# Finding eight top-512 thresholds in a fused attention and expert layer: scores turned so that a partition holds 256 scores of one expert

## The reference

```python
xf = z.reshape(-1, 256)                        # 4096 tokens
k = 4096 // 8                                  # 512 tokens for each of 8 experts
scores = (jnp.tanh(xf @ gate_w.T) + 1.0) * 0.5 # 4096 x 8, between 0 and 1
vals, idx = jax.lax.top_k(scores.T, k)         # for each expert its 512 highest scores
y = _layernorm(xf[flat_idx].reshape(k, n, d), ln_gamma, ln_beta)
h = gelu(einsum('knd,nfd->knf', y, fc1s) + b1s)
o = (einsum('knf,ndf->knd', h, fc2s) + b2s) * vals.T[:, :, None]
out = xf.at[flat_idx].add(o.reshape(k * n, d))
```

## Time and profile before

| | |
|---|---|
| median of 3 runs | 1595.7 us |
| profiled execution, its own time | 1597.86 us |
| span of its trace | 1596.1 us |
| PE busy | 1514.2 us (95%) |
| DVE busy | 1123.7 us (70%) |
| ACT busy | 910.7 us (57%) |
| POOL busy | 546.1 us (34%) |
| threshold rounds, first test to last | 1271.81 to 1304.93 us |
| mean granted PE clock | 0.965 |

### The profile page before, as it was taken

One profiled execution on the slowest core, in us unless ns is written; L12 is line 12 of the kernel. 1 busy time (PEld: TensorE's weight loads), 2 busy tenths in 40 slices (PEclk: granted clock), 3 DMA queues, 4 the chain that ended last, 5 costly groups with the idle time before them and its releaser, 6 DMA issues. The chain is left out here.

```text
span 1596.1 us, 26481 instructions
## 1 busy us (share of the span) xinstructions
PE 1514.2 (95%) x9025; PEld 733.7 (46%) x9025; DVE 1123.7 (70%) x3056; ACT 910.7 (57%) x1754; POOL 546.1 (34%) x1009
## 2 busy tenths in 40 slices
PE   8899999999999999999999999999999868999997
PEld 4433444444444444444444444444443424666664
DVE  6878887887787788778877877788781274554441
ACT  2167777677766777677777677777767301112111
POOL 4122333442343225233433442451121302443342
PEclk9599999999999999999999999999999877999999
DMA  6776662855376556737672855377300211343432
GB/s 136 155 135 104 127 88 77 121 105 106 104 104 136 87 101 124 123 84 109 120 122 83 115 105 105 94 102 141 42 3 3 87 38 38 101 108 100 123 90 50
DMA packets 82490, 155.46 MB, mean 97 GB/s; under 512 B 13012, under 2 KB 46420, under 8 KB 82356
## 3 DMA queue, kind: packets, MB, share of 16 engines
q1 hardware_dynamic: 76212, 145.25, 47.0%
q0 software_dynamic: 6144, 8.52, 3.1%
HBM read 96.52 MB, written 53.08 MB: 94 GB/s over the span
## 5 line engine op out<-in xcount | busy, mean ns | idle before, releaser
L829 ACT ACTIVATE probs<-bank_ps 128x512 f32<-128x512 f32 (+1 forms) x1408 | 730.1, 579 | 247.9 <-PE bank_ps L613 239.0
L920 DVE TENSOR_REDUCE chunk_max<-bank_ps 128x1 f32<-128x512 f32 x1024 | 653.5, 683 | 144.0 <-PE bank_ps L652 140.2
L652 PE MATMUL bank_ps<-k_stack,q_stack 62*128 62x512 f32 (+3 forms) x1536 | 536.3, 432 | 7.4 <-DVE chunk_max L920 4.1
L613 PE MATMUL bank_ps<-q_stack,k_stack 64*128 64x512 f32 (+3 forms) x1536 | 512.8, 423 | 25.7 <-ACT probs L829 22.1
L652 PEld LDWEIGHTS bank_ps<-k_stack,q_stack 62*128 62x128 f32 x1536 | 248.2, 191 | 372.4 <-DVE chunk_max L920 202.2
L923 DVE CUSTOM_DVE_ANT_0 masked<-bank_ps,causal 128x128 bf16<-128x128 f32 (+3 forms) x512 | 232.9, 485 | 62.4 <-PE bank_ps L652 58.8
L631 PE MATMUL out_ps<-probs,v_cross 128*32 128x512 f32 x2048 | 275.7, 610 | 0.0
L613 PEld LDWEIGHTS bank_ps<-q_stack,k_stack 64*128 64x128 f32 x1536 | 234.5, 189 | 83.2 <-ACT probs L829 76.3
L1093 POOL TENSOR_TENSOR pool_idle<-pool_idle 128x1 f32<-128x1 f32 x292 | 56.4, 193 | 582.5 <-ACT probs L829 386.1
L1406 ACT ACTIVATE h<-h_ps,b1T 128x512 f32<-128x512 f32 x64 | 44.0, 687 | 254.5 <-PE h_ps L1352 220.4
L1352 PE MATMUL h_ps<-ff_yT,w1T 128*128 128x512 f32 x256 | 122.6, 615 | 1.0 <-DVE ff_yT L1419 1.0
(11 more groups left out here) (165 smaller groups left out, 1384.0 us busy)
## 6 DMA issues: line engine op xcount, KB each, us to landing
parts_dram<-parts SPq DMA_DIRECT2D x70, 512.0 KB, 2.7
k_stack<-parts_dram SPq DMA_DIRECT2D x180, 192.0 KB, 11.6
q_stack<-parts_dram SPq DMA_DIRECT2D x180, 128.0 KB, 10.5
w1T<-in_L_ffn_fc1s SPq DMA_DIRECT2D x8, 1024.0 KB, 5.0
w2T<-in_L_ffn_fc2s SPq DMA_DIRECT2D x8, 1024.0 KB, 7.3
z_rows<-z_sb SPq DMA_DIRECT2D x8, 528.0 KB, 3.1
x_sb<-in_x SPq DMA_DIRECT2D x8, 512.0 KB, 3.8
ctxT<-in_ctx SPq DMA_DIRECT2D x8, 512.0 KB, 4.1
```

The lines of the kernel that those rows point to most:

```text
L613: mm = pe.matmul(bank_of(turn)[:, of.at:of.end], k_stack[base:base + SIDE, g, pair, of.keys:of.keys + P], q_stack[base:base + SIDE, g, pai ...
L652: return pe.matmul(bank[:, 0:n], q_stack[base:base + MAX_ROWS, g, pair, qc:qc + P], k_stack[base:base + MAX_ROWS, g, pair, k0:k0 + n], sta ...
L829: nc.scalar.activation(probs[:, buffer(u, i, p), side, columns], bank_of(("score", g, i, p, side))[:, columns], ACT.Exp, scale=SCALE)\
L920: nc.vector.tensor_reduce(dst, bank[:, 0:n], AX.X, ALU.max).then_inc(max_done, 1)
```

## The change: what it does

The scores are turned once, by two fp32 PE transposes of every second column of `s_all` and a DVE copy out of PSUM, into `by_expert`, in which a partition holds 256 scores of one expert and 16 neighbouring partitions hold one expert. A level is then one number a partition, and the three tests of a round are three DVE instructions of 256 elements, each with its level as a scalar per partition and each summing its own result into one column of `counts`. One PE product of three columns with `block_ones` (ones within blocks of 16 partitions) sums over an expert. `passed` compares with 511.5 and sums the three results (`passes`); `levels` and `bottom` follow from it. `levels_ahead`, the part of the next levels that does not need the count, is issued while PE works. At the end `bottom_wide` and a PE transpose turn the result back, and a copy picks `low`. The products of ones after the count are in 5 rounds in place of 13 (the eighth to the twelfth), and none follows the last count. The identity is no longer written again: the attention's tile is kept.

```diff
@@ attention(...), feed_forward(...): both take ident as an argument; in program():
+        ident = stack.enter_context(nc.sbuf_tensor("ident", [P, P], F32))
@@ feed_forward, shapes
-    TILE_STEP = 4
+    SHARE = P // E
+    VALUES = NTOK // SHARE
...
-        reached_ps = h_ps[:, 0, 0:TESTS * E * TILE_STEP]
+        by_expert_ps = transpose_ps[:, 0, 0:VALUES]
+        reached_ps = h_ps[:, 0, 0:TESTS]
+        low_ps = transpose_ps[:, 1, 0:P]
@@ tensor queue
+            flat_scores = s_all[:].rearrange("p e t -> p (e t)")
+            for c in range(VALUES // P):
+                mm = pe.transpose(by_expert_ps[:, c * P:(c + 1) * P], flat_scores[:, c::VALUES // P], ident[:])
+            mm.then_inc(turned, 1)
+            pe.wait_ge(consts, 1)
             pe.wait_ge(pool_set, 1)
             for r in range(ROUNDS):
                 pe.wait_ge(tested, r + 1)
-                for t in range(0, TILES, TILE_STEP):
-                    mm = pe.matmul(reached_ps, ones[:], reached[:, :, :, t:t + TILE_STEP], start=t == 0,
-                                   stop=t == TILES - TILE_STEP)
-                mm.then_inc(counted, 1)
-                multiply_ones(ONES_PER_ROUND)
+                pe.matmul(reached_ps, block_ones[:], counts[:], start=True, stop=True).then_inc(counted, 1)
+                if ROUNDS - ROUNDS_WITH_ONES <= r + 1 < ROUNDS:
+                    multiply_ones(ONES_PER_ROUND)
+            pe.wait_ge(bottom_set, ROUNDS + 1)
+            pe.transpose(low_ps, bottom_wide[:], ident[:]).then_inc(low_full, 1)
@@ vector queue (the old rounds are printed above, L1522 to L1548)
+            step = [0.5 * 0.25 ** r for r in range(ROUNDS + 1)]
+            nc.vector.memset(bottom[:], 0.0).then_inc(bottom_set, 1)
+            for n in range(TESTS):
+                nc.vector.memset(multiples[:, n:n + 1], n + 1.0)
+            for n in range(TESTS):
+                init = nc.vector.memset(levels[:, n:n + 1], (n + 1) * step[0])
+            init.then_inc(levels_set, 1)
+            dve.wait_ge(turned, 1)
+            nc.vector.tensor_copy(by_expert[:], by_expert_ps).then_inc(laid, 1)
+            dve.wait_ge(laid, 1)
             for r in range(ROUNDS):
+                dve.wait_ge(levels_set, r + 1)
+                for n in range(TESTS):
+                    test = nc.vector.tensor_scalar(reached[:, n, :], by_expert[:], levels[:, n:n + 1], None, ALU.is_ge,
+                                                   ALU.add, accum_out=counts[:, n:n + 1])
+                test.then_inc(tested, 1)
+                dve.wait_ge(bottom_set, r + 1)
+                nc.vector.scalar_tensor_tensor(out=levels_ahead[:], in0=multiples[:], scalar=step[r + 1],
+                                               in1=bottom[:].broadcast_to([P, TESTS]), op0=ALU.mult, op1=ALU.add)\
+                    .then_inc(ahead_set, 1)
                 dve.wait_ge(counted, r + 1)
+                nc.vector.tensor_scalar(passed[:], reached_ps, K - 0.5, None, ALU.is_ge, ALU.add, accum_out=passes[:])\
+                    .then_inc(passes_set, 1)
+                dve.wait_ge(passes_set, r + 1)
                 if r < ROUNDS - 1:
+                    dve.wait_ge(ahead_set, r + 1)
+                    nc.vector.scalar_tensor_tensor(out=levels[:], in0=passes[:].broadcast_to([P, TESTS]), scalar=step[r],
+                                                   in1=levels_ahead[:], op0=ALU.mult, op1=ALU.add).then_inc(levels_set, 1)
+                    nc.vector.scalar_tensor_tensor(out=bottom[:], in0=passes[:], scalar=step[r], in1=bottom[:],
+                                                   op0=ALU.mult, op1=ALU.add).then_inc(bottom_set, 1)
+                else:
+                    nc.vector.scalar_tensor_tensor(out=bottom_wide[:], in0=passes[:].broadcast_to([P, P]), scalar=step[r],
+                                                   in1=bottom[:].broadcast_to([P, P]), op0=ALU.mult, op1=ALU.add)\
+                        .then_inc(bottom_set, 1)
+            dve.wait_ge(low_full, 1)
+            nc.vector.tensor_copy(low[:], low_ps.rearrange("p (e n) -> p e n", e=E)[:, :, 0]).then_inc(low_set, 1)
+            dve.wait_ge(low_set, 1)
@@ GpSimd queue
-            nc.gpsimd.memset(ident[:], 0.0)
+            nc.gpsimd.memset(block_ones[:], 1.0)
...
             pool.wait_ge(pool_set, 1)
+            in_block = lambda sign: [[sign * SHARE, E], [0, SHARE]]
+            nc.gpsimd.affine_select(out=block_ones[:], in_=block_ones[:], compare_op=ALU.is_ge, fill=0.0, base=0,
+                                    pattern=in_block(-1), channel_multiplier=1).then_inc(block_step, 1)
+            pool.wait_ge(block_step, 1)
+            nc.gpsimd.affine_select(out=block_ones[:], in_=block_ones[:], compare_op=ALU.is_ge, fill=0.0, base=SHARE - 1,
+                                    pattern=in_block(1), channel_multiplier=-1).then_inc(consts, 1)
...
-            nc.gpsimd.affine_select(out=ident[:], in_=ident[:], compare_op=ALU.not_equal, fill=1.0, base=0,
-                                    pattern=[[-1, P]], channel_multiplier=1).then_inc(consts, 1)
@@ constants
-ONES_PER_ROUND = 4
+ONES_PER_ROUND, ROUNDS_WITH_ONES = 4, 5
```

More of the change, by code:

```diff
@@ L257, in head_place, with attention @@
     return SIDE * (h % SIDES), h // SIDES
-def attention(nc, x, ctx_in, w, z_rows, out, parts_dram, shift_dram, s_all, x1, z_sb, z_out, base_out):
+def attention(nc, x, ctx_in, w, z_rows, out, parts_dram, shift_dram, s_all, x1, z_sb, ident, z_out, base_out):
     B, T, C = x.shape
@@ L307, in attention @@
         minus_half = sb("minus_half", [P, NT])
-        ident = sb("ident", [P, P])
         causal = sb("causal", [P, T])
@@ L1202, in _, with feed_forward @@
             second_norm(B - 1)
-def feed_forward(nc, w, z_rows, out, s_all, z_out, base_out):
+def feed_forward(nc, w, z_rows, out, s_all, ident, z_out, base_out):
     E, C, F = w["fc1s"].shape
@@ L1246, in feed_forward @@
         pool_idle = sb("ff_pool_idle", [P, 17]); dve_idle = sb("ff_dve_idle", [P, 1])
-        ident = sb("ff_ident", [P, P])
+        block_ones = sb("block_ones", [P, P], BF16)
         ones = sb("ones", [P, P], BF16); upto = sb("upto", [P, P], BF16)
@@ L1250, in feed_forward @@
         token = sb("token", [P, 2, TILES], BF16)
-        low = sb("low", [P, E]); levels = sb("levels", [P, 1 + TESTS, E]); steps = sb("steps", [P, 1 + TESTS, E])
-        counts = sb("counts", [P, 1 + TESTS, E]); passed = sb("passed", [P, 1 + TESTS, E])
-        reached = sb("reached", [P, TESTS, E, TILES], BF16)
+        low = sb("low", [P, E])
+        by_expert = sb("by_expert", [P, VALUES]); reached = sb("reached", [P, TESTS, VALUES], BF16)
+        multiples = sb("multiples", [P, TESTS]); levels = sb("levels", [P, TESTS]); levels_ahead = sb("levels_ahead", [P, TESTS])
+        counts = sb("counts", [P, TESTS], BF16); passed = sb("passed", [P, TESTS]); passes = sb("passes", [P, 1])
+        bottom = sb("bottom", [P, 1]); bottom_wide = sb("bottom_wide", [P, P])
         count = sb("count", [P, E])
@@ L1275, in feed_forward @@
         above_ps = o_ps[:, 1, 0:E * TILES]
-        reached_ps = h_ps[:, 0, 0:TESTS * E * TILE_STEP]
+        by_expert_ps = transpose_ps[:, 0, 0:VALUES]
+        reached_ps = h_ps[:, 0, 0:TESTS]
+        low_ps = transpose_ps[:, 1, 0:P]
         w1_in = sem("w1_in"); w2_in = sem("w2_in"); b2_in = sem("b2_in"); small_in = sem("small_in")
-        consts = sem("ff_consts"); pool_set = sem("ff_pool_set")
-        tested = sem("tested"); counted = sem("counted"); round_step = sem("round_step")
+        consts = sem("ff_consts"); pool_set = sem("ff_pool_set"); block_step = sem("block_step")
+        turned = sem("turned"); laid = sem("laid"); low_full = sem("low_full")
+        tested = sem("tested"); counted = sem("counted"); levels_set = sem("levels_set")
+        bottom_set = sem("bottom_set"); ahead_set = sem("ahead_set"); passes_set = sem("passes_set"); low_set = sem("low_set")
         route = sem("route"); route_ps = sem("route_ps")
@@ L1519, in _ @@
             wide = lambda tile: tile[:].unsqueeze(2).broadcast_to([P, E, TILES])
[L1522 to L1528, removed]
-            for r in range(ROUNDS):
[L1530 to L1534, removed]
-                dve.wait_ge(counted, r + 1)
[L1536 to L1545, removed]
-                if r < ROUNDS - 1:
-                    nc.vector.tensor_tensor(levels[:], low[:].unsqueeze(1).broadcast_to([P, 1 + TESTS, E]), steps[:],
-                                            ALU.add).then_inc(round_step, 1)
@@ L1716, in program @@
         z_sb = stack.enter_context(nc.sbuf_tensor("z_sb", [P, T // P, C + E], F32))
+        ident = stack.enter_context(nc.sbuf_tensor("ident", [P, P], F32))
         z_out = stack.enter_context(nc.semaphore("z_out"))
         base_out = stack.enter_context(nc.semaphore("base_out"))
-        attention(nc, x, ctx_in, w, z_rows, out, parts_dram, shift_dram, s_all, x1, z_sb, z_out, base_out)
-        feed_forward(nc, w, z_rows, out, s_all, z_out, base_out)
```

(2 more changed lines are left out.)

## The result

The changed kernel takes 1587.99 us, the median of 5 runs (1583.82 to 1589.78), against 1595.7 us before (by then the median of 5 runs, and the same); the ratio is 0.9942 with a 95% interval from 0.9919 to 0.9964. Forecast was 1587.0 in a range from 1579 to 1594. Timed once more on another occasion beside 11 runs of the kernel before (median 1594.94), it took 1587.5 us, ratio 0.9949 (0.9934 to 0.9964). So the medians lie 7.4 and 7.7 us apart, on the edge of the 0.5% that one measurement can tell; the two intervals together reach from 5.7 to 12.9 us, and both exclude no change.

What follows compares the result with a forecast made beforehand. The threshold search was taken to bound the start of the feed-forward part, one for one. Start +0.64, twelve rounds -9.1, last test +0.3, tail -0.5 sum to -8.7 us: 1595.7 becomes 1587.0 us, range 1579 to 1594.

Steps and rivals of the forecast that it cites:

- The bound: Feed-forward start: ACT and POOL wait on the threshold search, whose time is added to the end one for one.
- Start: Block's start until the first test: two fp32 transposes and a PSUM copy delay it by 0.64 us.
- Three tests: DVE tests of each round: 1.28 us at one element per step, spacing 0.40 us, where one test took 0.96.
- Rival 1: Search tests take two elements per step: three take 0.89 us, -12.5 us in all, 1583.2 us; chance 0.24.
- One product and two small operations: Rest of each round behind the tests: product 0.28 us, passed 0.20, levels 0.19; bottom and levels_ahead are hidden.
- The allowance of 0.05 for one more wait: DVE's queue in each round: one additional wait, put at 0.05 us, bounds 0 and 0.1.
- Ones: PE products of ones in five rounds: cost nothing at 2.00 us a round, PE being free after about 1.85 us.
- Tail: From the end of the last test to count: 2.33 us against 2.83, that is -0.5 us.
- Sum: Whole kernel: +0.64 - 9.1 + 0.3 - 0.5 = -8.7 us, giving 1587.0 us on the median.
- Later clock effects: After the gather, transposes and first expert: PE's clock falling at another moment adds about 2.5 us on either side.
- The range: Whole kernel: 1579 us (tests at two elements, kind clock) to 1594 us (small operations not hidden, unkind clock).
- Rival 3: Search tests do not overlap and run slowly: three take 2.15 us, +2.6 us in all, 1598.3 us; chance 0.05.

Runs made afterwards that it cites:

- e2: Changed kernel with the three tests as plain comparisons without sums, counts constant: round 1.56 to 1.57 us, search 24.05 us; whole time not given.
- e4: Changed kernel with levels_ahead issued behind passed and bottom ahead of levels, so neither is covered: round 2.19 us, search 31.03 us; whole time not given.
- e7: Changed kernel with the turned scores in bf16, sums unused, counts constant: round 1.97 us; whole time not given.
- e8: Changed kernel with 44 products of ones ahead of the first transposes in place of 32, profiled: search 28.22 us; whole time not given.
- e9: Same kernel as e8 (changed kernel, 44 products of ones in place of 32), timed: 1588.26 us, ratio 0.9949 to the kernel before.
- e3: Changed kernel with a semaphore wait between the three tests of a round: round 2.22 us, search 31.93 us; whole time not given.
- e5: Changed kernel with four products of ones after each of the 13 counts: rounds 1.96 to 1.97 us, search 28.44 us; whole time not given.
- e1: Kernel before, unchanged, profiled again: search 35.00 us; whole time not given.
- e6: Kernel before without products of ones in its rounds: mean round 2.86 us, search 38.31 us; whole time not given.

## Why the prediction was right, and where it was off

*The bound.* Right: the search is added to the end one for one; POOL's and ACT's waits shrank by 9.0 us each, and no later wait swallowed it. In this pair the first expert took 0.9 us longer after (19.1 against 18.2), which is the clock effect below.

*Start.* Forecast +0.64 us. Measured first test 1.13 us into the block against 0.33: +0.80 us, and +0.61 in e2, e4, e7, e8 and e9 (0.94). The two transposes depend on the clock at that moment: one takes 0.28 to 0.36 us in e8 and 0.42 to 0.46 in the profile after. The step had one number for them, which is near that of the full clock.

*Three tests.* Forecast 1.28 us with a spacing of 0.40; measured 1.27 and 0.40. This step decided the sum, and the choice of the accumulating row over the quicker one was right. The rule of the Trainium skill (VectorE: DVE Perf Modes, "The perf-mode tier table") holds for the comparison without a sum, 348 ns in e2, and doesn't mention the one with a sum, which takes 475 ns in the same shape. Rival 1 thus priced a real rate, of the wrong operation. "The DRAIN you can't avoid" on the same page of the Trainium skill has the next operation wait until the pipe is empty, but adds that one which is not held starts earlier; the prediction took the first half alone. The trace agrees with the second: 0.40 us from start to start with operations of 0.475 us, and 0.52 with a wait in between (e3).

*One product and two small operations.* Forecast: `passed` 0.28 us behind the third test's end, measured 1290.28 - 1290.01 = 0.27 at the full clock and 0.30 in the second round, at the lower one. `levels` to the next test 0.19, measured 0.20; the round 2.00, measured 1.97. The allowance of 0.05 for one more wait was not needed: the pieces alone, 1.27 + 0.30 + 0.20 + 0.20, are 1.97.

*Ones.* Forecast: nothing at 2.00 us a round. Right: in the profile after the rounds with ones take 1.96 to 1.98 us like the others, and so do all twelve in e5 (1.96 to 1.97 behind the first). The 1.85 us they were to keep PE for are 1.73 in e2.

*Tail.* Forecast 2.33 us from last test to `count`, measured 1294.34 - 1291.97 = 2.37 by the chain.

*Sum.* Forecast -8.7 us against the profiled execution; between the two profiles the search shrank by 37.25 - 28.53 = 8.72 us. That the sum fits to 0.1 us is in part luck: the start cost 0.16 us more than forecast and the twelve rounds saved 9.4 us in place of 9.1. On the median the gain was 7.7 and then 7.4 us. The step that was off is the last one, "1595.7 - 8.7 = 1587.0 us": it took a gain that was read from one execution as that of the median. The profile said that the mean round held both clocks, and the forecast used that mean as fixed. The old search takes 35.0 us where most rounds are at 2.4 GHz, 37.2 as profiled, and 38.3 where all are at 1.2 (e1, before, e6); the new one took 28.2 to 28.5 us in all profiles with its computation unchanged. So between the profiled executions the gain is 6.5 to 9.0 us, by the clock that the old kernel happened to get, and the measured 7.4 to 7.7 us lie in it. How often it gets which is not known: two profiles are no distribution.

*Later clock effects* were put at 2.5 us on either side. From first product to `o_ps` the profiles show 16.2 to 19.1 us, of the size forecast; e9 shows that 12 more products of ones bring nothing. But from first product to the end the profiles of the table show 259.1 to 263.2 us, and this does not follow the first stretch: e8, with the shortest first stretch (16.2), and e5, with 19.0, have the two longest ends (244.3 and 244.2). Why is open.

*The range.* Its lower end does not follow from its terms: 1583.2 - 2.5 is 1580.7, not 1579. Nothing hangs on it here.

Open: why the attention's end moves between 1265 and 1275 us from one execution to another. No run was made for it; it is as large as the gain.

## What to carry to other kernels

Price an accumulating comparison from a row that accumulates: here the sum cost the quicker rate in fp32 (475 against 348 ns), bf16 values did not bring it back (476), and three short ones in a row overlapped by 0.08 us each as long as no wait stood between them. When an old stretch hangs on TensorE's clock, read it at both levels before subtracting it from a median, since the gain is then a range. A single profile of a version that is to beat another by 2 us proves nothing where executions differ by 7.

## What the hardware showed that was not expected

The quicker comparison without a sum, 348 ns alone, took up to 1090 ns while POOL wrote its constants, whereas the one with a sum took 473 to 480 ns in the same place (e2 against the profile after). Rival 3 had named a row of 637 ns of the quicker operation; it is the quicker operation that shows this slowness, and the one with a sum does not. In e2 it made the first round 2.46 us long against 1.56, a loss of 0.9 us once.
